# 14 of 49 target tiles of a graph convolution summed from gathered source rows instead of dense adjacency blocks, in both layers

## The reference

```python
def _gcn_layer(x, W, b, src, dst, norm, num_nodes):
    h = x @ W
    msg = h[src] * norm[:, None]
    agg = jax.ops.segment_sum(msg, dst, num_segments=num_nodes)
    return agg + b
...
src, dst, norm = _gcn_norm(edge_index, num_nodes)   # adds one more self loop, norm = dinv[src] * dinv[dst]
z = jax.nn.relu(_gcn_layer(x, W1, b1, src, dst, norm, num_nodes))
z = jax.nn.relu(_gcn_layer(z, W2, b2, src, dst, norm, num_nodes))
...
xn = _layernorm(x, axis=-1)
x = x + _L0_gnn_ref(xn, ...) + _L0_mix_ref(xn[None], ...)[0]      # mix: linear attention over all nodes
x = x + _L0_ffn_ref(_layernorm(x, axis=-1)[None], ...)[0]         # ffn: slice attention, 8 heads x 64 slices
```

## Time and profile before

| | |
|---|---|
| median of 3 runs | 2008.22 us |
| the profiled execution | 2019.06 us |
| its span | 2017.1 us |
| granted TensorE clock, mean | 0.963 of full speed |
| busy: PE, PE weight loads | 94%, 70% |
| busy: DVE, ACT, POOL | 59%, 42%, 15% |
| DMA: mean rate, queues' share | 125 GB/s, 35% of 16 engines |

### The profile page before, as it was taken

The page is one execution under the profiler, slowest core; times in us unless marked ns, Lnnn a source line. Parts: engine busy times, 40 slices in busy tenths (PEclk is TensorE's granted clock), DMA queues, the critical chain, the costliest instruction groups (busy, mean ns, idle before and its releaser), DMA issues. The chain is left out here.

```text
span 2017.1 us, 45282 instructions
## 1 busy us (share of the span) xinstructions
PE 1894.1 (94%) x18843; PEld 1415.6 (70%) x18843; DVE 1185.0 (59%) x2748; ACT 852.7 (42%) x1970; POOL 300.0 (15%) x417
## 2 busy tenths in 40 slices
PE   3598989999999999999979999999999999999598
PEld 3254555555555555555559999999999999998476
DVE  6788887666666666666605555555555555555322
ACT  1577765665656665666602222222222222222100
POOL 3133110000000000000021111111111111111033
PEclk7698999999999999999989999999999999999599
DMA  3133322223232222223254444444444444442087
GB/s 97 51 108 94 93 74 104 121 97 129 97 129 97 122 104 109 117 97 129 96 187 142 144 144 144 144 140 144 143 143 143 144 143 143 142 142 78 13 269 241
DMA packets 92702, 252.13 MB, mean 125 GB/s; under 512 B 14143, under 2 KB 59347, under 8 KB 79939
## 3 DMA queue, kind: packets, MB, share of 16 engines
q1 hardware_dynamic: 69225, 218.83, 30.4%
q10 hardware_dynamic: 21096, 25.65, 3.6%
q0 software_dynamic: 2176, 4.75, 0.9%
HBM read 131.99 MB, written 118.02 MB: 124 GB/s over the span
## 5 line engine op out<-in xcount | busy, mean ns | idle before, releaser
L1392 PE MATMUL ps<-hs,at 128*128 128x512 f16 x2401 | 669.8, 379 | 0.3 <-POOL at L1209 0.3
L1611 PE MATMUL ps<-at,big 128*128 128x128 f16 x9604 | 576.8, 219 | 7.0 <-DMA at<-at_scratch 7.0
L1611 PEld LDWEIGHTS ps<-at,big 128*128 128x128 f16 x9604 | 555.7, 98 | 34.6 <-issue 8.4
L1448 ACT CAST at<-ps 128x392 f16<-128x392 f32 x784 | 375.0, 486 | 289.5 <-PE ps L1353 274.1
L1353 PE MATMUL ps<-big 128*128 128x98 f16 x3136 | 471.6, 208 | 8.1 <-DVE big L1293 8.1
L1353 PEld LDWEIGHTS ps<-big 128*128 128x128 f16 x3136 | 297.8, 98 | 142.6 <-DVE big L1293 9.7
L1392 PEld LDWEIGHTS ps<-hs,at 128*128 128x128 f16 x2401 | 230.1, 97 | 149.0 <-issue 1.8
L1293 DVE TENSOR_TENSOR big<-iota_lo,key_lo 128x1024 f16<-128x1024 f16 x392 | 268.2, 684 | 0.0
L1293 DVE TENSOR_TENSOR big<-iota_hi,key_hi 128x784 f16<-128x784 f16 x392 | 218.9, 559 | 1.1 <-PE ps L1353 1.0
L1725 DVE SCALAR_TENSOR_TENSOR big<-ps,small,blogb 128x512 f32<-128x512 f32 x49 | 36.8, 751 | 231.0 <-PE ps L1647 231.0
L1828 POOL TENSOR_TENSOR key_lo<-key_lo,big 128x512 f32<-128x512 f32 (+1 forms) x49 | 61.9, 1264 | 706.4 <-ACT big L1786 706.4
(11 more groups left out here) (281 smaller groups left out, 2298.0 us busy)
## 6 DMA issues: line engine op xcount, KB each, us to landing
at_scratch<-at SPq DMA_DIRECT2D x49, 1568.0 KB, 5.2
at<-at_scratch SPq DMA_DIRECT2D x49, 1568.0 KB, 6.9
xT_scratch<-big SPq DMA_DIRECT2D x98, 128.0 KB, 2.0
big<-xT_scratch SPq DMA_DIRECT2D x49, 256.0 KB, 3.3
wT_scratch<-big ACTq DMA_DIRECT2D x49, 256.0 KB, 2.0
hs<-wT_scratch SPq DMA_DIRECT2D x49, 256.0 KB, 3.4
big<-in_x_dram SPq DMA_DIRECT2D x96, 128.0 KB, 2.4
x_scratch<-big ACTq DMA_DIRECT2D x48, 128.0 KB, 1.7
```

Source lines behind the costliest of these rows:

```text
L1392: mm = te.matmul(ps[:, 2 + b, :], lhsT=at[:, b, k * P:(k + 1) * P], rhs=hs[:, k, :], start=(k == 0), stop=(k == T - 1))
L1448: a.copy(to.rearrange("p k (i j) -> p k i j", j=WIN), ps[:, BANKS[m % len(BANKS)], 0:UW * KC].rearrange("p (i k j) -> p k i j", i=UW, j=WI ...
L1611: mm = te.matmul(ps[:, b, c * NT:(c + 1) * NT], lhsT=hs2[:, k, h * C + c * P:h * C + (c + 1) * P], rhs=at[:, b, k * P:(k + 1) * P], start= ...
```

## The change

Of each 7 target tiles 5 stay dense; two (tiles 2, 5, 9, 12, 16, ... 47; 14 in all, `LISTED`) are summed from a list of their edges instead. Each listed tile gets 36 chunks (`CH`) of 128 edges. For a chunk, POOL fetches the 128 source rows (1 KB each, from a copy of the table in DRAM) by one indirect DMA, DVE makes one-hots of the 128 targets (6 chunks in one TENSOR_TENSOR), and PE multiplies: in layer 1 one matmul of 512 columns, in layer 2 four of 128. One more step adds the self loops.

- Preparation: the first edge of each listed tile is found (7 short DVE instructions, 7 matmuls).
- Norms: SP stores the table `hs` to DRAM (49 DMAs more); POOL issues 28 more indirect DMAs for the edges' sources and targets, DVE makes 14 rows of keys from them.
- Layer 1: only the 35 dense tiles are built; their loop has 35 steps. The 504 chunks are laid along these steps, 15 in each (`PER`). POOL issues 15 fetches a step into a ring of 16 buffers, and between them, in the same order, `self_loops` and `lower`. PE's wait for the self loops moves from the first matmul of a tile to the one over its own block, which is now in the middle of the tile. ACT and PE have three banks for building instead of four. SP stores 35 blocks and the 49 tiles of the new table.
- Layer 2: 35 block loads instead of 49. POOL issues the 504 fetches into a ring of 32: for a listed tile the first 32 are spread over the POOL iterations since the listed tile before, the last 4 come at its own. DVE makes the 6 one-hot instructions of a listed tile after `split` of the tile two before it.

The core of the diff:

```diff
+        CH = 36
...
+        LISTED = [7 * g + 2 + 3 * k for g in range(TG) for k in range(2)]
+        DENSE = [t for t in range(T) if t not in LISTED]
+        NL, ND = len(LISTED), len(DENSE)
+        NCH = NL * CH
...
+                def gather_ids(j):
+                    place = first_edge[:, j % 2, j // 2:j // 2 + 1]
+                    for to, of in ((edge_src, src_dram), (edge_dst, dst)):
+                        pool.indirect_dma_start(
+                            out=to[:, j, :], out_offset=None, in_=of.rearrange("(e a) -> e a", a=1),
+                            in_offset=bass.IndirectOffsetOnAxis(ap=place, axis=0)).then_inc(ids_landed, 16)
...
+        MSGS, MSG_SEMS, HOTS_AT_ONCE, HOT_RING = 16, 4, 6, 3
+        PER = 15
...
+                def self_loops(d):
+                    pool.wait_ge(at_stored, (d + 1) * UNITS)
+                    block_t = at[:, d % 2, DENSE[d] * P:(DENSE[d] + 1) * P]
+                    g.tensor_tensor(block_t, block_t, ident16[:, :], ALU.add).then_inc(looped, 1)
...
+                def fetch(c):
+                    if c >= MSGS:
+                        pool.wait_ge(edges_used, c - MSGS + 1)
+                    pool.indirect_dma_start(
+                        out=msg[:, c % MSGS, :], out_offset=None, in_=h1_dram,
+                        in_offset=bass.IndirectOffsetOnAxis(ap=edge_src[:, c // CH, c % CH:c % CH + 1], axis=0)
+                        ).then_inc(landed[c // (MSGS // MSG_SEMS) % MSG_SEMS], 16)
+                def tile(d, b, u):
+                    for i in range(PER):
+                        if (d + 1) * PER + i < NCH:
+                            fetch((d + 1) * PER + i)
+                        if i == 1 and 0 <= d < ND:
+                            self_loops(d)
+                        if i == 4 and late(d - 2) is not None:
+                            lower(late(d - 2))
+                        if i == 13 and early(d - 1) is not None:
+                            lower(early(d - 1))
+                pipeline(tile, ND, 2, lead=1, lag=2)
...
-                                pe.wait_ge(agg_ready, t - 1)
-                        mm = te.matmul(ps[:, 2 + b, :], lhsT=at[:, b, k * P:(k + 1) * P], rhs=hs[:, k, :],
-                                       start=(k == 0), stop=(k == T - 1))
-                        if k == T - 1:
+                            pe.wait_ge(at_stored, (d + 1) * UNITS)
+                            if d >= 2:
+                                pe.wait_ge(agg_ready, late(d - 2) + 1)
+                        if k == DENSE[d]:
+                            pe.wait_ge(looped, d + 1)
+                        mm = te.matmul(ps[:, 2 + d % 2, :], lhsT=at[:, d % 2, k * P:(k + 1) * P], rhs=hs[:, k, :],
+                                       start=(n == 0), stop=(n == T - 1))
...
+                def add_edges(c):
...
+                    if c % (MSGS // MSG_SEMS) == 0:
+                        pe.wait_ge(landed[c // (MSGS // MSG_SEMS) % MSG_SEMS], landed_count(c, MSGS // MSG_SEMS, MSGS))
+                    if c % HOTS_AT_ONCE == 0:
+                        pe.wait_ge(edge_hot_ready, c // HOTS_AT_ONCE + 1)
+                    i = c % HOTS_AT_ONCE
+                    mm = te.matmul(ps[:, bank, :],
...
+                                   .rearrange("p (q k r) -> p q k r", k=P, r=2)[:, i // 2, :, i % 2],
+                                   rhs=msg[:, c % MSGS, :], start=(c % CH == 0), stop=False)
+                    mm.then_inc(edges_used, 1)
+                    if c % CH == CH - 1:
+                        te.matmul(ps[:, bank, :], lhsT=ident16[:, :], rhs=hs[:, LISTED[j], :], start=False, stop=True
+                                  ).then_inc(summed, 1)
+                def turn(n):
+                    pe.wait_ge(agg_ready, n + 1)
...
+                def sum_listed(t, b, i):
+                    j = LISTED.index(t)
+                    n = j * CH + i
+                    if i == 0:
+                        pe.wait_ge(aggT_ready, t - 1 + T)
+                    if n % PER_SEM == 0 or i == 0:
+                        pe.wait_ge(landed[n // PER_SEM % MSG_SEMS], landed_count(n, PER_SEM, MSGS2))
+                    if i % HOTS_AT_ONCE == 0:
+                        pe.wait_ge(edge_hot_ready, NCH // HOTS_AT_ONCE + n // HOTS_AT_ONCE + 1)
+                    m = i % HOTS_AT_ONCE
+                    for h in range(2):
+                        for c in range(CB):
+                            mm = te.matmul(ps[:, b, c * NT:(c + 1) * NT], lhsT=msg2[:, n % MSGS2, h * C + c * P:h * C + (c + 1) * P],
+                                           rhs=edge_hot[:, i // HOTS_AT_ONCE, :]
+                                           .rearrange("p (q k r) -> p q k r", k=P, r=2)[:, m // 2, :, m % 2],
+                                           start=(i == 0 and h == 0 and c == 0), stop=False, skip_group_check=True)
+                    mm.then_inc(edges_used, 1)
+                    if i == CH - 1:
+                        for h in range(2):
+                            for c in range(CB):
+                                mm = te.matmul(ps[:, b, c * NT:(c + 1) * NT], lhsT=hs2[:, t, h * C + c * P:h * C + (c + 1) * P],
+                                               rhs=ident16[:, :], start=False, stop=(h == 1), skip_group_check=True)
...
-                            sum_tile(t, b, u, k)
+                    listed = t in LISTED
+                    steps = CH if listed else T
+                    places = (1, 3, 30, 35, 35) if listed else (3, 6, 31, 37, 44)
+                    for k in range(steps):
+                        if listed:
+                            sum_listed(t, b, k)
+                        elif reached(t, 0) and within(t, T):
+                            sum_tile(t, b, k)
...
+                def edge_hots(t):
+                    j = LISTED.index(t)
+                    if j >= 1:
+                        dve.wait_ge(edges_used, NCH + j * CH)
...
                         divide(t, b)
                         split(t, b)
+                        if t + 2 in LISTED:
+                            edge_hots(t + 2)
...
+                def fetched_in(c):
+                    j, i = c // CH, c % CH
+                    if i >= MSGS2:
+                        return LISTED[j]
+                    begin = LISTED[j - 1] if j else 0
+                    return begin + i * (LISTED[j] - begin) // MSGS2
+                def fetch(c):
+                    if c >= MSGS2:
+                        pool.wait_ge(edges_used, NCH + c - MSGS2 + 1)
+                    pool.indirect_dma_start(
+                        out=msg2[:, c % MSGS2, :], out_offset=None, in_=h2_dram,
+                        in_offset=bass.IndirectOffsetOnAxis(ap=edge_src[:, c // CH, c % CH:c % CH + 1], axis=0)
...
                         g.tensor_tensor(base_in[:, b, :], base_in[:, b, :], bvo, ALU.add).then_inc(biased, 1)
+                    for c in range(NCH):
+                        if fetched_in(c) == t + 2:
+                            fetch(c)
```

More of the change, by code:

```diff
@@ L223, in gps_layer @@
             bvb = take([P, CB, P])
+            pick = take([GW, GW // (2 * SUPER), P])
+            starts = take([P, T])
+            first_f = take([P, 2, TG])
+            listed_len = take([1, 2, TG])
+            longest = take([1, 2])
             bpart = take([1, 3, 2 * C], BF16)
@@ L467, in _ @@
                 pe.wait_ge(wprod_used, 2)
+                pe.wait_ge(starts_ready, 1)
+                for r in range(GW // (2 * SUPER)):
+                    mm = t.matmul(ps[:, 2, r * TG:(r + 1) * TG], lhsT=pick[:, r, :], rhs=wlo_f[:, :, 0], start=True, stop=True)
+                mm.then_inc(starts_spread, 1)
                 pe.wait_ge(deg_loaded, 16)
@@ L597, in gps_layer @@
             keyh = take([GW, 2, WPS, CAP])
+            edge_dst = take([P, NL, CH], I32)
             take = carve(big_f[:, 0:KEYS_AT])
@@ L1339, in _ @@
                 v.tensor_copy(kx, ps[:, 4:6, 0:C + 3]).then_inc(kx_kept, 1)
-                pipeline(tile, T, 2, lead=1, lag=1)
+                pipeline(tile, ND, 2, lead=1, lag=2)
             @block.tensor
@@ L1418, in tile @@
-                        if i == 20 and reached(t, 1):
-                            turn(t - 1, 1 - b)
-                        if i == 36 and reached(t, 1):
-                            multiply(t - 1, 1 - b)
+                        if reached(t, 0) and within(t, ND):
+                            aggregate(t, range(i * (T - ALONE) // WPT, (i + 1) * (T - ALONE) // WPT))
+                        if (t, i) in chunks_at:
+                            add_edges(chunks_at[t, i])
+                        for at_i, do, n in ((20, turn, early(t - 1)), (32, multiply, early(t - 1)),
+                                            (44, turn, late(t - 1)), (58, multiply, late(t - 1))):
+                            if i == at_i and n is not None:
+                                do(n)
@@ L1525, in gps_layer @@
         final_rest = hs_f32[:, HB * C + C:]
```

(7 more changed lines are left out.)

324 lines of the change are left out of this document (206 added, 118 removed).

## The result

The changed kernel takes 2641.5 us (median of 4 runs, 2636.2 to 2645.0) against 2008.4 us (4 runs, 2004.2 to 2013.7): ratio 1.314, 95% interval 1.311 to 1.317. The forecast was 2166 us, its range ended at 2290. The direction was right; 475 us were missing, and layer 2 accounts for more than all of them: it was forecast 48 us longer and is 553 us longer.

What follows compares the result with a forecast made beforehand. PE's own work bounds both layers before; POOL's fetches bound layer 1 after. Layer 1 +103, layer 2 +48 and the rest +6 make 157 us on 2019.06, 2176 profiled; less 10.8, 2166 us, range 2020 to 2290.

Steps and rivals of the forecast that it cites:

- Layer 1, PE's saving (-78): Layer 1, PE's side: 35 dense steps plus chunks and self loops take 638 us in place of 716, 78 less.
- Layer 1, POOL (+103): Layer 1: POOL becomes the bound, a step of 24.1 us against PE's 18.2, so the layer takes 103 us more.
- the end of one instruction: Layer 1: a fetch's list read waits until one DVE instruction ends, 0.12 us extra a fetch; 0.20 was taken.
- 385 + 497 S: Layer 1's end in us, S being the distance of two POOL fetches; S = 1.50 gives 1130.5, +103 us.
- busy or issuing all through it: Expected sign in the profile after: POOL is busy or issuing through all of layer 1.
- wait for POOL at the self loops: Expected sign in layer 1: PE waits for POOL at the self loops, some 5 us a step.
- Layer 2, shorter tiles (-37.5): Layer 2: a listed tile has 148 matmuls in place of 196, saving 37.5 us over 14 tiles.
- one-hots (+43.4): Layer 2: each listed tile's first matmul waits 3.1 us for DVE's one-hots behind `split`, 14 times, +43.4 us.
- Layer 2, fetches (+17, +25): Layer 2: PE waits for late landings, 2.5 us in every second listed tile (+17), and at the stage's start (+25).
- The rest (+6): Outside the layers' main work: last table store before the barrier +3 us, 21 short DVE instructions before layer 1 +3.
- A to D: Four cases for kernel time, in order: 2075 to 2275 us (chance 0.55), 2025 to 2071 (0.23), 2317 (0.10), 1963 (0.12).
- C: Layer 1: POOL starves through whole DVE bursts, fetches 1.79 us apart, layer 1 +248, kernel 2317 us; chance 0.10.

Runs made afterwards that it cites:

- the pauses: Changed kernel with POOL waiting in layer 2 after every third fetch until it has landed, all 504 fetches kept: 2477.02 us.
- the wide matmuls: Changed kernel with half as many matmuls and weight loads in layer 2's dense tiles, each of 256 columns instead of 128, fetches kept: 2546.04 us.

## Why the prediction was right in direction and wrong in size

**Layer 1, PE's saving (-78).** Right: 76 us, in the run without fetches.

**Layer 1, POOL (+103).** Near in size, in part by luck: the last `lower` ended at 1093.6, not 1130.5, so +66. An undisturbed fetch of 128 rows costs nearly what one of 112 did, 0.95 + 0.30 = 1.25 us, where I had added 0.06 for the rows. The mean is 1.07 + 0.30 = 1.37 us, so 0.12 on top in place of my 0.20; that is the bound that I had given for "the end of one instruction" of DVE, though no run here takes DVE's part away:

```profile
L1319 POOL DMA_INDIRECT big<-h_scratch,edge_src x504 | 539.4, 1070 | 181.9 <-issue 115.0 <-PE ps L1539 58.2 <-remote 8.7
```

By the forecast's own 385 + 497 S an S of 1.37 gives +39. The mechanism wasn't the one I described either. POOL was not "busy or issuing all through it": it waited 58 us for PE to use up messages. PE had no wait for POOL at the self loops, the sign I had named. Its idle was starving and waits for ACT and DVE, the three rows above, and ACT was held up itself. POOL's row and the starving both come from the same fetches, and no run here splits the 144 us between them.

**Layer 2, shorter tiles (-37.5) and one-hots (+43.4).** The wait was 46.4 us in 14 waits, and taking it away gave 39 us. Without fetches layer 2 spanned 860.0 us, 37 more than before, where these two terms say +6. The trace of that run shows most of the missing 31 us, by the distance from one start to the next. The waits are 3 us longer. A listed tile's matmuls are 0.062 us apart and not 0.0558: 13 us. `mix`, which comes right behind the wait, takes 98.9 us in place of 87.3, and the granted clock is 0.50 for 3.4 us or more behind 9 of the 14 waits. Dense matmuls take 3 to 4 us more. Why a listed matmul costs 0.060 even at the full clock isn't shown.

**Layer 2, fetches (+17, +25).** This is the step that failed. I charged a fetch to POOL, and to PE only where it would wait for a landing. PE waited for no landing, and the fetches cost 516 us (1375.8 less 860.0). I wrote "POOL keeps up on average", which was true and not the question. I bounded the distance of two fetches but never asked what a row of them does to the other engines. The trace of before could not show it: the twelve pairs stand in two rows of seven. Beside the first, in the 10 us from 17 on, PE executed 47 matmuls and 45 weight loads, fewer than it gets through before it starves; beside the second it had nothing to do; and the later fetches come singly. So the cost should have been called unbounded. The direction doesn't hang on this step: without any fetch in layer 2 the kernel takes 2131.65 us, still more than before.

**The rest (+6)** and the rivals: the seam between the layers is 7.7 us longer, where I had 3; layer 1's sums begin no later than before (303.9 and 305.1 us). None of A to D has a starved PE; C came nearest in time, for another reason. (The sum itself gives 2165 us, not 2166.)

What the pauses and the wide matmuls show is that PE is short of instructions in a row of indirect fetches. What inside the chip holds them up isn't shown, and it isn't PE's supply alone, since ACT is late too. Two causes the trace rules out. It isn't a late block of instructions from memory: in the 3 us ahead of the slow stretch at 1646 the instruction queue shows

```profile
q8 instruction: 1, 0.02, 2.0%
```

and in the 9 us from 1646 on nothing. At the stage's start it is plainer. From 1125 to 1165 PE executes 53 matmuls in 40 us, the instruction packets before and after this time are 46 us apart, and the only queue that moves anything is that of the fetches themselves:

```profile
q0 software_dynamic: 1440, 3.93, 34.7%
```

This rules out the loads of dense blocks as a second culprit as well: none is under way in these 40 us. One packet of 16 KB goes with some 250 instructions of PE (137 packets for 17121 matmuls and as many loads). The Trainium skill (Runtime: NRT & Kernel Launch, Instruction fetch mechanics) says that instructions come in blocks of 16 KiB, fetched ahead, so that crossing into a new one is mostly hidden. The trace agrees on the size of the blocks, and the starving comes without a crossing.

## What to carry to other kernels

Price a new kind of instruction on every engine, not on its own alone, and where the trace shows it only singly, measure one long row of it beside the engine that bounds the kernel before building on it. Here the cheap test (the listed tile's fetches added, or taken out) would have shown 1 us of PE for each fetch. If indirect transfers must run beside a PE that issues short matmuls, put them in rows of two or three with a pause until they have landed, give PE few wide instructions meanwhile, and check that the pauses don't make it wait for the data: here they did, and no form beat the kernel before.

## What the runs showed of the hardware

- Indirect transfers in a row follow each other at 1.25 us with 128 rows of 1 KB and at 1.14 us with 16 rows; plain ones from POOL take 0.54 us each.
- In a row of them PE executes 100 to 140 more instructions at full rate in layer 2, then one to three matmuls per us, until about 2 us after the last. In layer 1 ACT's copies start up to 4.95 us late as well. Plain transfers of the same bytes do nothing of the kind, from POOL in either layer or from SP in layer 2.
- Waiting for the landing after every third fetch made a kernel 164 us faster.
- In 1646 to 1654 PE is busy for 3.03 of 8 us; the granted clock falls to 0.50 in this time and stays there for 5 us after PE is fully busy again. Of the 516 us that layer 2's fetches cost, 300 are more idle and 188 more busy time of the same matmuls.
